# Attention: reciprocals of the softmax denominators taken once per value, in a 128x16 tile filled and spread by DMAs

## The chip, the core and the metric

The kernel runs on one NeuronCore of a Trainium2 chip. Its time is the device time of one execution in microseconds; three executions of the kernel before gave a median of 2079.34 us (2077.96 to 2079.47). A profile is of one execution, recorded by the hardware profiler. Engines: PE (TensorE: matmuls), DVE (VectorE), ACT (ScalarE), POOL (GpSimd), SP (SyncE, which here only issues DMAs).

## The reference

Two layers over x of shape (4, 1024, 512). The first is an adaptive-layernorm block with two MLPs. The second, cut to what matters here:

```python
h = _sln(hidden, w, ...)                                  # layernorm, scaled by the condition
q, k, v = ...                                             # 16 heads of 32, from h @ Wqkv.T + bqkv
energy = jnp.einsum('bhqd,bhkd->bhqk', q, k)              # 1024 x 1024 for each head and batch
att = jax.nn.softmax(energy, axis=-1) / D ** 0.5
out = jnp.einsum('bhqk,bhkd->bhqd', att, v)
out = out @ Wp.T + bp ; h1 = out + hidden ; return _sln(h1, ...) + h1
```

The softmax denominator of a query is one number for each head; the output of that query and head has 32 values, and all are divided by that one number.

## The kernel before

Five stages follow each other: setup, the first layer, the q/k/v projections, attention, and the output projection. Attention takes the stretch from about 950 to 1917 us. It works through 16 groups (4 batches x 4 groups of HG = 4 heads; 4 heads x 32 dimensions fill the 128 partitions). A group has STEPS = 16 steps: 2 halves of 512 queries, and in each half 8 blocks of 128 keys. Groups 1 to 12 run in a loop of 4 turns of 3 groups; the others are written out.

In a step PE makes four energy tiles (keys x queries, line 1149) in two PSUM banks, ACT takes their exponential (line 1278), and PE multiplies the one-step-older exponentials with v (line 1161, `av`). POOL adds the exponentials of two steps (line 1389, `pair`), and PE sums them over the keys with a stationary block of ones, 32 columns wide (line 1176, `den`): so each denominator stands 32 times, once for each of the 32 partitions of its head.

Beside it runs the search for the row maxima of queries that come later: 32 units to a group, two in each step. For a unit PE makes energies with queries on the partitions (line 1133, two matmuls of 512 keys) into one of two PSUM buffers `e_ps`, and DVE reduces them to a maximum (line 1305, `take_max`). Before the first matmul of unit n, PE waits until DVE has done unit n-2 (`pe.wait_ge(max_done, n - 1)`, line 1132). I call the two units of step i "ia" and "ib". The order is written out by hand: in an odd step PE also runs the first matmul of the next step's first unit (lines 1194 and 1195), behind the step's last energy tile. The units of steps 0 to 2 finish the group's own second half, those from step SWITCH = 3 belong to the next group. After them the maxima are negated, turned by PE and ACT, and put by two small DMAs as two more rows of the q stack (`place_neg`, line 1082).

At the end of a half ACT copies the sum of av to SBUF (`take_av`, line 1256), and later the denominators (`take_den`, line 1263: step 2 of the next group for half 1, step 10 for half 0). DVE inverts them in eight pieces of 128x64, one a step (`invert`, line 1324), between the step's two maxima. POOL multiplies (`finish`, line 1376), before pairs 1 and 5 of the next group, and SP stores the result to DRAM (`store`, line 1086).

All these DMAs go out on SP's one queue. In a group g, SP waits for the last av of group g-1 (in step 0), then issues ten loads for group g+2 (`load_group`: `load_stack` lines 90 and 94, nine DMAs, and v, line 1075; 3.5 MB; groups 1 to 13 only), then place_neg for half 1, store of half 0, place_neg for the next group's half 0, store of half 1. Group 15 loads the output projection's first inputs instead.

Of the kernel before, what the change touches and what calls it, by code (L numbers as in the profile page):

```python
# [6 lines left out]
P = 128  # L7
# [3 lines left out]
H, HD = 16, 32  # L11
KT = D // P
FT = FF // P
CH = 512
NCH = T // CH
TT = CH // P
G = B * KT
# [955 lines left out]
def attention_stage(nc, sh, wp_t):  # L973
# [11 lines left out]
    with ExitStack() as ctx:  # L985
        def sb(name, shape, dt=F32):
            return ctx.enter_context(nc.sbuf_tensor(name, shape, dt))

        def sem(name):
            return ctx.enter_context(nc.semaphore(name))  # L990
# [4 lines left out]
        LEAD = 13  # L995
        SWITCH = STEPS - LEAD
        TURN = (SWITCH + KC, SWITCH)
        PIECES = KC
        PC = CH // PIECES

        sh.projection_tiles = [t for t in early(nc, *PROJECTION_TILES) if "gap" not in t.name]
        sb("at_stacks_place", [P, 2 * RING * HG * N])
# [5 lines left out]
        av_sb = sb("at_av_sb", [P, QH, CH])  # L1008
        den_sb = sb("at_den_sb", [P, QH, CH])
        rden = sb("at_rden", [P, QH, CH])  # L1010
        out = sb("at_out", [P, QH, CH])
        mrow = sb("at_mrow", [P, QH, UNITS])
        neg = sb("at_neg", [P, 2, UNITS])
# [11 lines left out]
        av_done, av_taken = sem("at_av_done"), sem("at_av_taken")  # L1025
        pair_ready = sem("at_pair_ready")
        den_done, den_taken = sem("at_den_done"), sem("at_den_taken")
        rden_ready = sem("at_rden_ready")
        out_ready = sem("at_out_ready")
        wp_loaded, wp_split = sem("at_wp_loaded"), sem("at_wp_split")  # L1030

# [8 lines left out]
        def halves(g, h):  # L1040

            return QH * g + h + 1
# [25 lines left out]
        @block.sync  # L1068
        def _(sp):
            def load_group(g, slot):  # L1070
                load_stack(sp, sh, qs, ks, g, slot)
                load_v(g, slot)

            def load_v(g, slot):
                sp.dma_start(v[:, slot], sh.v_d[g]).then_inc(stack_loaded[slot], 16)

            def place_neg(g, slot, half):

                sp.wait_ge(negt_taken, halves(g, half))
                for part in range(2):  # L1080
                    dst = qs[96 + part:97 + part, slot, half].bitcast(F32).rearrange("o j (c q) -> o (j c) q", q=P)
                    sp.dma_start(dst, neg_t[part * UNITS:(part + 1) * UNITS, :]).then_inc(negm_loaded, 16)

            def store(g, half):
                sp.wait_ge(out_ready, halves(g, half))
                sp.dma_start(sh.at_d[g, :, half * CH:(half + 1) * CH], out[:, half]).then_inc(out_free[half], 16)

            def group(g, slot, nth=None, first=False, load=True, with_next=True):
                if not with_next:

                    sp.wait_ge(av_done, STEPS * g)
                    for half in range(QH):

                        sp.wait_ge(out_free[half], 16 * (KT + 1))
                    x, st = sh.projection_tiles[1], sh.projection_tiles[3]
                    for half in range(QH):
                        load_projection_input(sp, sh, a_f, x, st, 0, half)
                if not first and load:

                    sp.wait_ge(av_done, STEPS * g)  # L1100
                    load_group(g + 2, (slot + 2) % RING)
                place_neg(g, slot, 1)
                if not first:
                    store(g - 1, 0)
                if with_next:
                    place_neg(g + 1, (slot + 1) % RING, 0)
                if not first:
                    store(g - 1, 1)


            load_v(0, RING - 1)
            load_group(1, 0)
            place_neg(0, RING - 1, 0)
            load_group(2, 1)
            groups(sp, group)
            for half in range(QH):
                store(G - 1, half)

            for half in range(QH):
                sp.wait_ge(sh.a_loaded[half], 16 * KT)  # L1120
                sp.wait_ge(sh.x_loaded[half], 16)
                sp.wait_ge(sh.st_loaded[half], 32)
# [119 lines left out]
        def _(act):  # L1242
# [15 lines left out]
            def take_den(g, half):  # L1258
                act.wait_ge(den_done, KC // 2 * halves(g, half))
                if not (isinstance(g, int) and g == 0):  # L1260

                    act.wait_ge(rden_ready, PIECES * (halves(g, half) - 2))
                nc.scalar.copy(den_sb[:, half], den_ps[:]).then_inc(den_taken, 1)  # L1263

            def group(g, slot, nth=None, first=False, load=True, with_next=True):
# [36 lines left out]
        def _(dve):  # L1302
# [10 lines left out]
                dve.wait_ge(neg_ready, 2 * halves(g, half) - 1)  # L1313
                nc.vector.scalar_tensor_tensor(neg[:, LO, :], mrow[:, half], -1.0, neg[:, HI, :], ALU.mult, ALU.subtract).then_inc(neg_ready, 1)

            def invert(g, half, piece):

                if piece == 0:
                    dve.wait_ge(den_taken, halves(g, half))
                    if not (isinstance(g, int) and g == 0):  # L1320

                        dve.wait_ge(out_ready, halves(g, half) - 2)
                cols = slice(piece * PC, (piece + 1) * PC)
                nc.vector.reciprocal(rden[:, half, cols], den_sb[:, half, cols]).then_inc(rden_ready, 1)  # L1324

            def group(g, slot, nth=None, first=False, load=True, with_next=True):
                for i in range(STEPS):
                    units = units_of_step(g, slot, i, with_next)
                    for unit in units[0:1]:
                        take_max(*unit)  # L1330

                    if i >= 12:
                        for piece in ([i - 12] if with_next else [2 * (i - 12), 2 * (i - 12) + 1]):
                            invert(g, 0, piece)
                    elif not first:
                        invert(g - 1, *((1, i - 4) if i >= 4 else (0, i + 4)))
                    for unit in units[1:2]:
                        take_max(*unit)
                    if not with_next and KC // 2 <= i < KC // 2 + 2 * KT:

                        half, k = divmod(i - KC // 2, KT)
                        dve.wait_ge(sh.a_hi, KT * half + k + 1)
                        nc.vector.tensor_tensor(a_s[:, half, LO, k], a_f[:, half, k], a_s[:, half, HI, k].bitcast(F32),
                                                ALU.subtract).then_inc(sh.a_lo_last if k == KT - 1 else sh.a_lo, 1)
                    if i == TURN[1] - 1:
                        negate_max(g, 1)
                    if with_next and i == TURN[0] - 1:
                        negate_max(g + 1, 0)
# [8 lines left out]
                if n == UNITS - 1:  # L1357
                    negate_max(0, 0)
            groups(dve, group)
            for piece in range(PIECES):  # L1360
                invert(G - 1, 1, piece)

            dve.wait_ge(rden_ready, PIECES * halves(G - 1, 1))
            dve.wait_ge(av_taken, halves(G - 1, 1))
            dve.wait_ge(out_free[1], 16 * G)
            dve.wait_ge(out_ready, halves(G - 1, 0))
# [2 lines left out]
        @block.gpsimd  # L1369
        def _(pool):  # L1370
            def finish(g, half):
                pool.wait_ge(av_taken, halves(g, half))
                pool.wait_ge(rden_ready, PIECES * halves(g, half))

                pool.wait_ge(out_free[half], 16 * (g + 1))
                nc.gpsimd.tensor_tensor(out[:, half], av_sb[:, half], rden[:, half], ALU.mult).then_inc(out_ready, 1)

            def group(g, slot, nth=None, first=False, load=True, with_next=True):

                for pair in range(PAIRS if with_next else PAIRS - 1):  # L1380
                    if pair in (1, 5) and not first:
                        finish(g - 1, pair // 4)

                    pool.wait_ge(exp_done, HG * (STEPS * g + 2 * pair + 2))
                    if not (first and pair < 2):

                        pool.wait_ge(den_done, PAIRS * g + pair - 1)
                    a = 2 * pair % 4
                    nc.gpsimd.tensor_tensor(psum2[:, pair % 2], probs[:, a], probs[:, a + 1], ALU.add).then_inc(pair_ready, 1)  # L1389


            nc.gpsimd.memset(ks[96:98, 0:RING - 1].bitcast(F32), 1.0).then_inc(ones_ready, 1)
            pool.wait_ge(ones_ready, 1)
            pool.wait_ge(wp_split, 1)
            nc.gpsimd.tensor_tensor(sh.wp[:, LO], wp_raw[:], sh.wp[:, HI].bitcast(F32), ALU.subtract)
            groups(pool, group)
            finish(G - 1, 0)
# [234 lines left out]
def build(nc, x, cond_t, ada_w, wg_t, wb_t, row_bias, lngb, colpack, biasrows, neg_mask, ident, w1, w2, fw1, fw2, wqkv, wp_t, y,  # L1632
          stages=5):

    with ExitStack() as ctx:
# [11 lines left out]
        sh.bias_rows = sb("bias_rows", [2, D], F32R)  # L1647
        sh.minus_half = sb("minus_half", [P, TT])
        sh.eps = sb("eps", [P, 2, TT])
        sh.act_passed, sh.dve_passed, sh.pe_passed = (ctx.enter_context(nc.semaphore(f"{e}_passed")) for e in ("act", "dve", "pe"))  # L1650
        sh.biasrows_in = biasrows
        sh.rows_d = nc.dram_tensor("rows_scratch", [len(SPREAD), B, D], F32, kind="Internal").ap()
        sh.x2_d = nc.dram_tensor("x2_scratch", [T, D], F32, kind="Internal").ap()

        sh.qk_d = nc.dram_tensor("qk_scratch", [2, 2, G, P, N], F32, kind="Internal").ap()
        sh.v_d = nc.dram_tensor("v_scratch", [G, P, KC, P], F32, kind="Internal").ap()
        sh.at_d = nc.dram_tensor("attn_scratch", [G, P, N], F32, kind="Internal").ap()

        weights = [w1.rearrange("(k p) n -> p k n", p=P), w2.rearrange("(k p) n -> p k n", p=P)]
# [78 lines left out]
```

## Time and profile before

| | us |
|---|---|
| median of 3 runs | 2079.34 (2077.96 to 2079.47) |
| span of the profiled execution, first to last instruction | 2077.5 |
| PE busy / DVE busy / POOL busy / ACT busy | 1964.5 / 1383.0 / 1105.7 / 855.7 |
| the reciprocals, line 1324 | 136.8 |

The profiled execution has no time of its own beside its span; the span lies 1.8 us under the median. "Busy" is the time in which an engine worked on an instruction. Matmuls overlap each other, so their start times say more than their durations.

### The profile page before, as it was taken

What the parts mean: (1) busy time and instruction counts of PE and PEld (TensorE: products, weight loads), DVE (VectorE), ACT (ScalarE), POOL (GpSimd) and SP (SyncE); (2) the same over time, 40 slices, a digit from 0 to 9 for tenths busy, and PEclk for the clock granted to TensorE, in tenths of its full rate; (3) what the DMA queues carried; (4) which work ended last, traced back from release to release, by engine and by line L of the source; (5) the groups of instructions that cost most, each with busy time, mean ns of one, the idle gap of its engine ahead of it and who ended that gap; (6) DMA issues with size and microseconds to landing.
All of it is one profiled execution on the core that took longest, in us unless ns stands there. A gap on an engine that the chain in (4) does not pass through costs nothing. (4 is left out here: it accounts for less than half of the span.)

```text
span 2077.5 us, 29213 instructions
## 1 busy us (share of the span) xinstructions
PE 1964.5 (95%) x9504; PEld 1203.7 (58%) x9504; DVE 1383.0 (67%) x1754; ACT 855.7 (41%) x1469; POOL 1105.7 (53%) x553
## 2 busy tenths in 40 slices
PE   6599999999998999989999999999999999998974
PEld 1488888888887888864444444444444444442652
DVE  3555665566455544447788778778777878876678
ACT  1323112311222222214666566656656666665212
POOL 0675556555652121223666666666665666665655
PEclk9799999999999999987999999999999999999987
DMA  7300101110125554664332133333213333021454
GB/s 238 111 31 22 51 30 40 30 50 20 31 102 183 177 187 177 207 186 93 77 82 49 41 83 77 82 83 74 51 47 83 77 83 83 11 83 59 139 166 147
DMA packets 104341, 189.24 MB, mean 91 GB/s; under 512 B 8186, under 2 KB 25722, under 8 KB 104220
## 3 DMA queue, kind: packets, MB, share of 16 engines
q1 hardware_dynamic: 85472, 176.71, 29.6%
q10 hardware_dynamic: 18560, 10.94, 1.8%
q8 instruction: 71, 1.16, 0.2%
q14 instruction: 46, 0.38, 0.1%
q0 software_dynamic: 192, 0.05, 0.0%
HBM read 119.99 MB, written 67.16 MB: 90 GB/s over the span
## 5 line engine op out<-in xcount | busy, mean ns | idle before, releaser
L1305 DVE TENSOR_REDUCE at_mrow<-banks 128x1 f32<-128x1024 f32 x512 | 614.7, 1222 | 198.1 <-PE banks L1133 198.1
L1389 POOL TENSOR_TENSOR at_pair<-at_probs 128x2048 f32<-128x2048 f32 x127 | 581.3, 4577 | 294.6 <-ACT at_probs L1278 294.6
L1278 ACT ACTIVATE at_probs<-banks 128x512 f32<-128x512 f32 x1024 | 556.9, 595 | 329.2 <-PE banks L1149 321.6
L1149 PE MATMUL banks<-early_qs,early_ks 98*128 98x512 f32 x1024 | 454.5, 447 | 11.3 <-issue 8.7
L1149 PEld LDWEIGHTS banks<-early_qs,early_ks 98*128 98x128 f32 x1024 | 193.0, 190 | 397.9 <-ACT at_probs L1278 350.5
L1133 PE MATMUL banks<-early_ks,early_qs 96*128 96x512 f32 x1024 | 399.0, 415 | 6.3 <-PEq L726 3.5
L1161 PE MATMUL banks<-at_probs,at_v 128*32 128x512 f32 x2048 | 276.2, 612 | 0.9 <-ACT at_probs L1278 0.9
L1133 PEld LDWEIGHTS banks<-early_ks,early_qs 96*128 96x128 f32 x1024 | 199.0, 197 | 46.4 <-DVE at_mrow L1305 19.5
L66 PE MATMUL banks<-l_ht,l_weights 128*128 128x512 f32 x768 | 178.8, 392 | 5.6 <-ACT l_gt L546 5.6
L66 PE MATMUL banks<-qk_nt,l_weights 128*128 128x512 f32 x768 | 177.1, 392 | 3.0 <-ACT qk_gt L861 3.0
L546 ACT ACTIVATE l_gt<-banks,mod 128x512 f32<-128x512 f32 x64 | 48.1, 777 | 313.9 <-PE banks L440 278.1
L66 PE MATMUL banks<-l_weights,l_hf 128*128 128x512 f32 x768 | 177.2, 390 | 0.0
L66 PEld LDWEIGHTS banks<-l_ht,l_weights 128*128 128x128 f32 x768 | 144.5, 189 | 35.8 <-issue 6.0
L66 PEld LDWEIGHTS banks<-qk_nt,l_weights 128*128 128x128 f32 x768 | 145.2, 189 | 33.5 <-ACT qk_gt L861 3.2
L66 PEld LDWEIGHTS banks<-l_weights,l_hf 128*128 128x128 f32 x768 | 143.7, 188 | 29.5
L1324 DVE RECIPROCAL at_rden<-at_den_sb 128x64 f32<-128x64 f32 x256 | 136.8, 539 | 14.2 <-ACT at_den_sb L1263 14.2
L1176 PE MATMUL banks<-at_pair,at_ones_col 128*32 128x512 f32 x1016 | 135.7, 606 | 0.0
L960 POOL TENSOR_TENSOR qk_nt<-qk_gt,qk_nt 128x512 fp32r<-128x512 f32 x32 | 43.0, 1362 | 156.3 <-DVE qk_nt L912 156.3
L870 ACT ACTIVATE qk_out<-banks,cols 128x512 fp32r<-128x512 f32 x64 | 44.1, 690 | 192.5 <-PE banks L66 186.4
L672 POOL TENSOR_TENSOR l_ht<-l_gt,l_ht 128x512 fp32r<-128x512 f32 x64 | 84.1, 1314 | 63.1 <-DVE l_ht L588 63.1
L588 DVE CAST l_ht<-l_gt 128x512 fp32r<-128x512 f32 x64 | 52.0, 812 | 90.3 <-ACT l_gt L555 49.0
L555 ACT ACTIVATE l_gt<-banks,cols 128x512 f32<-128x512 f32 x96 | 64.6, 688 | 105.0 <-POOL l_hf L672 51.0
(124 smaller groups left out, 2069.4 us busy)
## 6 DMA issues: line engine op xcount, KB each, us to landing
qk_scratch<-qk_out SPq DMA_DIRECT2D x64, 512.0 KB, 2.9
early_ks<-qk_scratch SPq DMA_DIRECT2D x48, 512.0 KB, 6.7
early_qs<-qk_scratch SPq DMA_DIRECT2D x96, 256.0 KB, 11.3
v_scratch<-qk_v ACTq DMA_DIRECT2D x32, 256.0 KB, 2.4
at_v<-v_scratch SPq DMA_DIRECT2D x16, 512.0 KB, 14.9
attn_scratch<-at_out SPq DMA_DIRECT2D x32, 256.0 KB, 2.3
o_a<-attn_scratch SPq DMA_DIRECT2D x32, 256.0 KB, 6.4
o_x<-x_scratch SPq DMA_DIRECT2D x8, 1024.0 KB, 7.4
```

The source lines that it names most:

```text
L66: last = pe.matmul(out, stationary(a), moving(b), start=start and n == 0, stop=stop and n == len(TERMS) - 1)
L555: nc.scalar.activation(gt[:, n % 2, :], halves[n][:], func, bias=sh.cols[:, col + m:col + m + 1]).then_inc(gt_full, 1)
L588: nc.vector.tensor_copy(dst[:, HI, i, :], gt[:, i % 2, :]).then_inc(gt_hi, 1)
L672: nc.gpsimd.tensor_tensor(dst[:, LO, i, :], gt[:, i % 2, :], dst[:, HI, i, :].bitcast(F32), ALU.subtract).then_inc(gt_lo, 1)
L1133: pe.matmul(e_ps[u % 2][:, keys, :], qs[0:96, slot, half, j, c * P:(c + 1) * P], ks[0:96, slot, j, keys * CH:(keys + 1) * CH], start=True, ...
L1149: pe.matmul(et[j % 2][:], ks[0:98, slot, j, (i % KC) * P:(i % KC + 1) * P], qs[0:98, slot, i // KC, j, :], start=True, stop=True).then_inc ...
L1161: last = pe.matmul(av_ps[rows, :], v[:, slot, kc, rows], probs[:, kc % 4, j, :], start=kc == 0, stop=kc == KC - 1)
L1176: last = pe.matmul(den_ps[rows, :], ones_col[:], psum2[:, pair % 2, j, :], start=n == 0, stop=n == KC // 2 - 1)
L1278: nc.scalar.activation(probs[:, i % 4, j, :], et[j % 2][:], ACT.Exp).then_inc(exp_done, 1)
L1305: nc.vector.tensor_reduce(mrow[:, half, u:u + 1], e_ps[u % 2], AX.XY, ALU.max).then_inc(max_done, 1)
L1324: nc.vector.reciprocal(rden[:, half, cols], den_sb[:, half, cols]).then_inc(rden_ready, 1)
L1389: nc.gpsimd.tensor_tensor(psum2[:, pair % 2], probs[:, a], probs[:, a + 1], ALU.add).then_inc(pair_ready, 1)
```

## The change

The denominators no longer are inverted in all their 32 copies. From `den_sb` a DMA takes one row of each head (4 rows of 512 values) and lays them out as 128 partitions x 16 values (`den_c`). DVE inverts this tile with one instruction. SP stores it to DRAM, waits until it has landed there, and loads it back with four DMAs, each of which writes a head's 512 values to 32 partitions of `rden`. The order on SP, DVE and POOL changes with it. The last half of the last group is inverted whole, without DMAs.

```diff
+        DEN_STEP = 2
+        ROWS = P // HG
+        DW = CH // ROWS
...
+            def spread_den(g, half):
+                sp.wait_ge(den_taken, halves(g, half))
+                if not (isinstance(g, int) and g == 0):
+                    sp.sem_inc(sh.sp_passed, 1)
+                    sp.wait_ge(rden_ready, halves(g, half) - 2)
+                sp.sem_inc(sh.sp_passed, 1)
+                sp.dma_start(den_c[:, half],
+                             den_sb[0:P:HD, half].rearrange("j (r c) -> j r c", c=DW)).then_inc(den_spread[half], 16)
+
+            def widen_rden(g, half):
+                first = isinstance(g, int) and g == 0
+                sp.wait_ge(rden_ready, halves(g, half))
...
+                sp.dma_start(sh.rden_d[half].rearrange("j (r c) -> (j r) c", c=DW), rden_c[:, half]).then_inc(rden_stored[half], 16)
+                sp.wait_ge(rden_stored[half], 16 * (g + 1))
...
+                    sp.wait_ge(out_ready, halves(g, half) - 2)
...
+                for j in range(HG):
+                    sp.dma_start(rden[HD * j:HD * (j + 1), half],
+                                 sh.rden_d[half, j].partition_broadcast(HD)).then_inc(rden_loaded[half], 16)
...
                     sp.wait_ge(av_done, STEPS * g)
                     load_group(g + 2, (slot + 2) % RING)
+                if not first:
+                    store(g - 1, 0)
+                    spread_den(g - 1, 1)
                 place_neg(g, slot, 1)
                 if not first:
-                    store(g - 1, 0)
+                    widen_rden(g - 1, 1)
+                    store(g - 1, 1)
+                spread_den(g, 0)
                 if with_next:
                     place_neg(g + 1, (slot + 1) % RING, 0)
-                if not first:
-                    store(g - 1, 1)
-
+                widen_rden(g, 0)
...
 # ACT, take_den
-                    act.wait_ge(rden_ready, PIECES * (halves(g, half) - 2))
+                    act.wait_ge(den_spread[half], 16 * g)
...
 # DVE
-            def invert(g, half, piece):
...
-                nc.vector.reciprocal(rden[:, half, cols], den_sb[:, half, cols]).then_inc(rden_ready, 1)
+            def invert(g, half):
+                dve.wait_ge(den_spread[half], 16 * (g + 1))
+                if not (isinstance(g, int) and g == 0):
+                    dve.wait_ge(rden_stored[half], 16 * g)
+                nc.vector.reciprocal(rden_c[:, half], den_c[:, half]).then_inc(rden_ready, 1)
 
                 for i in range(STEPS):
-                    units = units_of_step(g, slot, i, with_next)
-                    for unit in units[0:1]:
+                    for unit in units_of_step(g, slot, i, with_next):
                         take_max(*unit)
-
-                    if i >= 12:
-                        for piece in ([i - 12] if with_next else [2 * (i - 12), 2 * (i - 12) + 1]):
-                            invert(g, 0, piece)
-                    elif not first:
-                        invert(g - 1, *((1, i - 4) if i >= 4 else (0, i + 4)))
-                    for unit in units[1:2]:
-                        take_max(*unit)
+                    if i == DEN_STEP + 2 and not first:
+                        invert(g - 1, 1)
+                    if i == KC + DEN_STEP + 2:
+                        invert(g, 0)
...
-            for piece in range(PIECES):
-                invert(G - 1, 1, piece)
+            nc.vector.reciprocal(rden[:, 1], den_sb[:, 1]).then_inc(rden_ready, 1)
...
 # POOL, finish and group
-                pool.wait_ge(rden_ready, PIECES * halves(g, half))
+                pool.wait_ge(rden_loaded[half], 16 * HG * (g + 1))
...
-                    if pair in (1, 5) and not first:
-                        finish(g - 1, pair // 4)
+                    if pair == 3 and not first:
+                        finish(g - 1, 1)
+                    if pair == PAIRS - 1:
+                        finish(g, 0)
```

## Rows read from the trace of the kernel before

**Rows 1.** The page, busy time of each engine: us (share of the span) xinstructions.
```profile
PE 1964.5 (95%) x9504; PEld 1203.7 (58%) x9504; DVE 1383.0 (67%) x1754; ACT 855.7 (41%) x1469; POOL 1105.7 (53%) x553
```
**Rows 2.** Busy times by stretch; a plain group, then one with the loop's turn.
```profile
1253.00:1312.00 59.00, 59.00 (x326) 25.53 (x322) 47.48 (x53) 37.00 (x71) 39.03 (x11) 1.00 0.32 73
1371.00:1435.00 64.00, 61.88 (x322) 26.57 (x322) 46.90 (x52) 36.93 (x70) 38.88 (x10) 0.95 0.29 68
```
**Rows 3.** Waits, PE's and DVE's, 1000 to 1910 us: total, times, longest.
```profile
PE banks L1149 <- issue: 8.7, 3, 3.1
PE banks L1149 <- ACT at_probs L1278: 2.5, 6, 0.5
DVE at_mrow L1305 <- PE banks L1133: 180.5, 321, 3.0
```
**Rows 4.** The page's groups of instructions: busy, mean ns | idle before, releaser.
```profile
L1305 DVE TENSOR_REDUCE at_mrow<-banks 128x1 f32<-128x1024 f32 x512 | 614.7, 1222 | 198.1 <-PE banks L1133 198.1
L1324 DVE RECIPROCAL at_rden<-at_den_sb 128x64 f32<-128x64 f32 x256 | 136.8, 539 | 14.2 <-ACT at_den_sb L1263 14.2
```
**Rows 5.** Timeline, loads of group 5, then group 6: start, duration, engine, line.
```profile
1254.15 1.36 SPq L90 DMA_DIRECT2D early_ks<-qk_scratch  x3
...
1313.26 1.37 SPq L90 DMA_DIRECT2D early_ks<-qk_scratch  x3
1317.78 0.38 SPq L1075 DMA_DIRECT2D at_v<-v_scratch  x1
1322.69 0.58 ACT L1263 COPY at_den_sb<-banks 128x512 f32<-128x512 f32 x1 [0.73 <-PE banks L1176]
1329.05 1.22 DVE L1305 TENSOR_REDUCE at_mrow<-banks 128x1 f32<-128x1024 f32 x1 [0.38 <-PE banks L1133]
1331.19 1.23 DVE L1305 TENSOR_REDUCE at_mrow<-banks 128x1 f32<-128x1024 f32 x1 [0.92 <-PE banks L1133]
1332.89 0.64 PE L1133 MATMUL banks<-early_ks,early_qs 96*128 96x512 f32 x2
1333.86 4.58 POOL L1389 TENSOR_TENSOR at_pair<-at_probs 128x2048 f32<-128x2048 f32 x1 [2.47 <-ACT at_probs L1278]
```
**Rows 6.** DMA issues of group 6 by line, and their landing times from issue.
```profile
L1075 SPq DMA_DIRECT2D at_v<-v_scratch x1: 381/381/381, 1317.8 to 1317.8; - x1
DMA to landing us min/median/max: 13.5/13.5/13.5
L1082 SPq DMA_DIRECT2D early_qs<-at_neg_t x2: 508/545/582, 1326.6 to 1327.1; - x2
DMA to landing us min/median/max: 4.9/5.4/5.9
L1086 SPq DMA_DIRECT2D attn_scratch<-at_out x1: 430/430/430, 1327.9 to 1327.9; - x1
DMA to landing us min/median/max: 5.4/5.4/5.4
```
**Rows 7.** The same small DMAs and store in group 14, which loads nothing.
```profile
L1082 SPq DMA_DIRECT2D early_qs<-at_neg_t x2: 502/546/590, 1810.3 to 1810.8; - x2
DMA to landing us min/median/max: 1.8/1.8/1.8
L1086 SPq DMA_DIRECT2D attn_scratch<-at_out x1: 578/578/578, 1811.5 to 1811.5; - x1
DMA to landing us min/median/max: 2.2/2.2/2.2
```
**Rows 8.** Timeline at a turn of the loop, in the attention.
```profile
1373.12 0.79 PE L1149 MATMUL banks<-early_qs,early_ks 98*128 98x512 f32 x1 [2.64 <-issue]
1374.70 1.94 PE L1161 MATMUL banks<-at_probs,at_v 128*32 128x512 f32 x8
1376.99 1.38 SPq L90 DMA_DIRECT2D early_ks<-qk_scratch  x3
```
**Rows 9.** Timeline at the end of attention, DVE.
```profile
1911.85 3.43 DVE L1324 RECIPROCAL at_rden<-at_den_sb 128x64 f32<-128x64 f32 x8 [14.22 <-ACT at_den_sb L1263]
```

More of the change, by code:

```diff
@@ L997, in attention_stage @@
         TURN = (SWITCH + KC, SWITCH)
-        PIECES = KC
-        PC = CH // PIECES
+        DEN_STEP = 2
+        ROWS = P // HG
+        DW = CH // ROWS
         sh.projection_tiles = [t for t in early(nc, *PROJECTION_TILES) if "gap" not in t.name]
@@ L1010, in attention_stage @@
         rden = sb("at_rden", [P, QH, CH])
+        den_c = sb("at_den_c", [P, QH, DW])
+        rden_c = sb("at_rden_c", [P, QH, DW])
         out = sb("at_out", [P, QH, CH])
@@ L1027, in attention_stage @@
         den_done, den_taken = sem("at_den_done"), sem("at_den_taken")
+        den_spread = [sem(f"at_den_spread{i}") for i in range(QH)]
         rden_ready = sem("at_rden_ready")
+        rden_stored = [sem(f"at_rden_stored{i}") for i in range(QH)]
+        rden_loaded = [sem(f"at_rden_loaded{i}") for i in range(QH)]
         out_ready = sem("at_out_ready")
@@ L1082, in place_neg @@
                     sp.dma_start(dst, neg_t[part * UNITS:(part + 1) * UNITS, :]).then_inc(negm_loaded, 16)
+            def spread_den(g, half):
[10 more added lines that the diff above has]
+                if not first:
+                    sp.sem_inc(sh.sp_passed, 1)
+                    sp.wait_ge(rden_loaded[half], 16 * HG * g)
+                sp.sem_inc(sh.sp_passed, 1)
+                sp.dma_start(sh.rden_d[half].rearrange("j (r c) -> (j r) c", c=DW), rden_c[:, half]).then_inc(rden_stored[half], 16)
+                sp.wait_ge(rden_stored[half], 16 * (g + 1))
+                if not first:
+                    sp.sem_inc(sh.sp_passed, 1)
+                    sp.wait_ge(out_ready, halves(g, half) - 2)
+                sp.sem_inc(sh.sp_passed, 1)
+                for j in range(HG):
+                    sp.dma_start(rden[HD * j:HD * (j + 1), half],
+                                 sh.rden_d[half, j].partition_broadcast(HD)).then_inc(rden_loaded[half], 16)
             def store(g, half):
@@ L1101, in group @@
                     load_group(g + 2, (slot + 2) % RING)
+                if not first:
+                    store(g - 1, 0)
+                    spread_den(g - 1, 1)
                 place_neg(g, slot, 1)
                 if not first:
-                    store(g - 1, 0)
+                    widen_rden(g - 1, 1)
+                    store(g - 1, 1)
+                spread_den(g, 0)
                 if with_next:
                     place_neg(g + 1, (slot + 1) % RING, 0)
-                if not first:
-                    store(g - 1, 1)
+                widen_rden(g, 0)
             load_v(0, RING - 1)
@@ L1314, in negate_max @@
                 nc.vector.scalar_tensor_tensor(neg[:, LO, :], mrow[:, half], -1.0, neg[:, HI, :], ALU.mult, ALU.subtract).then_inc(neg_ready, 1)
-            def invert(g, half, piece):
[L1318 to L1323, printed above, removed]
-                nc.vector.reciprocal(rden[:, half, cols], den_sb[:, half, cols]).then_inc(rden_ready, 1)
+            def invert(g, half):
[3 more added lines that the diff above has]
+                nc.vector.reciprocal(rden_c[:, half], den_c[:, half]).then_inc(rden_ready, 1)
             def group(g, slot, nth=None, first=False, load=True, with_next=True):
                 for i in range(STEPS):
-                    units = units_of_step(g, slot, i, with_next)
-                    for unit in units[0:1]:
+                    for unit in units_of_step(g, slot, i, with_next):
                         take_max(*unit)
-                    if i >= 12:
-                        for piece in ([i - 12] if with_next else [2 * (i - 12), 2 * (i - 12) + 1]):
-                            invert(g, 0, piece)
-                    elif not first:
-                        invert(g - 1, *((1, i - 4) if i >= 4 else (0, i + 4)))
-                    for unit in units[1:2]:
-                        take_max(*unit)
+                    if i == DEN_STEP + 2 and not first:
+                        invert(g - 1, 1)
+                    if i == KC + DEN_STEP + 2:
+                        invert(g, 0)
                     if not with_next and KC // 2 <= i < KC // 2 + 2 * KT:
@@ L1359, in _ @@
             groups(dve, group)
-            for piece in range(PIECES):
-                invert(G - 1, 1, piece)
-            dve.wait_ge(rden_ready, PIECES * halves(G - 1, 1))
+            dve.wait_ge(den_taken, halves(G - 1, 1))
+            dve.wait_ge(out_ready, halves(G - 1, 1) - 2)
+            nc.vector.reciprocal(rden[:, 1], den_sb[:, 1]).then_inc(rden_ready, 1)
+            dve.wait_ge(rden_ready, halves(G - 1, 1))
             dve.wait_ge(av_taken, halves(G - 1, 1))
@@ L1649, in build @@
         sh.eps = sb("eps", [P, 2, TT])
-        sh.act_passed, sh.dve_passed, sh.pe_passed = (ctx.enter_context(nc.semaphore(f"{e}_passed")) for e in ("act", "dve", "pe"))
+        sh.act_passed, sh.dve_passed, sh.pe_passed, sh.sp_passed = (ctx.enter_context(nc.semaphore(f"{e}_passed")) for e in ("act", "dve", "pe", "sp"))
         sh.biasrows_in = biasrows
@@ L1656, in build @@
         sh.v_d = nc.dram_tensor("v_scratch", [G, P, KC, P], F32, kind="Internal").ap()
+        sh.rden_d = nc.dram_tensor("rden_scratch", [QH, HG, CH], F32, kind="Internal").ap()
         sh.at_d = nc.dram_tensor("attn_scratch", [G, P, N], F32, kind="Internal").ap()
```

## The prediction, made before the changed kernel was run

> **What bounds the kernel now.** I read the page's busy times first: PE works 95% of the span, DVE 67% [rows 1]. A busy share is an average, so I looked at attention alone. In a plain group PE is busy all of its 59 us at full clock, DVE 47 of them [rows 2]. The waits say it more sharply: from 1000 to 1910 us PE waits 8.7 us in three pieces for "issue", at the loop's three turns back, and 2.5 us for ACT; no wait for DVE is among them, while DVE waits 180 us for PE [rows 3]. So PE sets the pace, and DVE has time to spare: on average, not at any moment. The units of maxima hang together in both directions, through two PSUM buffers. What matters is how late DVE may be in one place before PE stops. A stop of PE isn't made good, as it has no idle time in which to catch up.
>
> **The work removed.** The 256 pieces are 136.8 us of DVE, with 0.43 us from start to start where they follow each other (8 in 3.43 us) [rows 4, 9]. Thirty-one of the 32 halves are now inverted by one 128x16 instruction. Per column a piece costs 0.43/64 = 0.007 us; 48 columns fewer than its 0.54 us give 0.54 - 0.32 = 0.22 us [rows 4, 9]; I take that. DVE is relieved of about 125 us. All of it lies beside PE's work, so it's worth nothing until PE waits for DVE. The cover is safe: PE has no wait that this DVE work ended. At attention's very end the 8 pieces are on the path; one 128x512 instruction at the same rate per column is the same 3.4 us, at most 0.3 less. I count 0.
>
> **The wait added, where it costs.** DVE now waits at step 4 of group g for the DMA that lays out the denominators of (g-1, half 1). Queued behind the waiting instruction on DVE are the maxima from 5a on; PE waits for those. Times of group 6 [rows 5, 6]:
> - The ten loads start at 1313.26, the last (v) is issued at 1317.78 and lands 13.5 us later, at 1331.3. The queue is full until then.
> - ACT has the denominators in SBUF at 1322.69 + 0.58 = 1323.3, so SP issues the layout there. Ahead of it in the same queue are the loads and, new, the store of half 0 (256 KB), which used to come after place_neg.
> - What does a small DMA do behind that queue? The two of place_neg, 8 KB each, were issued at 1326.6 and 1327.1 and landed 4.9 to 5.9 us later, both near 1332.0 to 1332.5; with nothing ahead they land in 1.8 us [rows 7]. So they did wait for the loads. The store behind them landed at 1327.9 + 5.4 = 1333.3.
> - The layout now stands behind loads and store. Lower bound: both store and layout move in no time, 1332.5. Upper bound: the store's 1333.3 and 0.9 us more for 128 pieces of 64 bytes, 1334.2. No row shows such small pieces; I take 1333.2, next to the store's landing, because the place in the queue is that of the store, and both small DMAs that stood before it are gone.
> - DVE is there at 1329.05 + 1.22 = 1330.3. It inverts at 1333.2 and is free at 1333.4, where 5a started at 1331.19: 2.2 us late. 5a then ends at 1334.65.
> - PE needs 5a for the first matmul of 6a, the second of the two from 1332.89 on, which started at about 1333.13. It now starts at 1334.65: a stop of 1.5 us. Bounds: 0.8 us by 1332.5, 2.5 us by 1334.2.
>
> The Trainium skill ("DMA: Bandwidth & Descriptors", section "Why a DMA increments its semaphore by 16 and not by 1") says that a DMA runs on as many of the 16 engines as divide the outermost dimensions of both sides. By it the layout (4 rows to 128 partitions) has 4 engines, each with 32 pieces, and is slower in itself than a transfer on all 16; the sum would lean to its upper end. No row here shows a DMA on four engines.
>
> **How often.** Groups 1 to 13 load. Place_neg's landing, counted from its issue, hardly differs in eleven of them (5.8 to 6.3 us against 5.9 here); in groups 7 and 13 it was about 1 us earlier. So 13 x 1.5 = 19.5, less about 1.5: 18 us. Group 14 has an empty queue: store 2.2 us, small DMA 1.8 us [rows 7], landed before DVE comes, 7 us after the denominators (1330.3 against 1323.3 [rows 5]). In group 15 no maxima are left to take after step 2; DVE's wait there holds only the splitting of the projection's input. I count 0 for both, with 1 us of doubt.
>
> **What else moves, at nothing.** Half 0: its layout is issued at step 10 into a queue that has long been empty, and lands 1.8 to 2.5 us later, while DVE comes two steps (7.4 us) after. Place_neg is now behind up to one store and one layout, some 1 to 2 us later, and is needed only at step 8, over 10 us after group 6's 1332.5. The widening for half 1: inverse at 1333.4, store to DRAM 0.4 + 2.2, four issues of 0.45 and a landing of 2.3, ready near 1340.3. POOL's pair 2 runs to 1333.86 + 4.58 = 1338.4 [rows 5], and pair 3 can't start before step 7's exponentials near 1341 (or 1342.5 with PE's stop): `finish`, 1.3 us, fits to within 1 us. ACT needs pair 3 only at step 10. SP's longer list delays nobody: its next urgent work is the loads at the next group's step 0, and widening half 0 is over some 5 us before. If that cover were gone, the price is the overrun itself, once a group.
>
> **The sum.** 2077.5 + 18 = 2095.5 for the profiled execution; the median lies 1.8 above the span, giving 2097.5, say 2098 us.
>
> **The rivals.**
> 1. *PE's clock falls with the stops* (chance 0.17). At the loop's turn PE stopped for 2.64 us and then ran its av of 8 matmuls in 1.94 us instead of 1.06; the stretch's granted clock is 0.95 [rows 2, 8]. From group 5's loads to group 6's it is 59.1 us, from group 6's (1313.26) to the turn's (1376.99) 63.7 [rows 5, 8]: 4.6 more, of which 2.6 are the stop, so the low clock (1.2 instead of 2.4 GHz) cost 2.0. If each stop brings this, 13 x (1.5 + 2.0) less 2 gives 43 us: 2122. Against it: my stop is half as long, and the only ones followed by a low clock in attention are the turns. It decides where stops come to 2.5 us. The Trainium skill ("TensorE: Matmul & The Clock Gate", "What's actually happening") has the low clock as PE's default, which activity lifts: by that rule a PE busy before and behind a stop of 1.5 us can keep its clock, and the sum stays at 2098.
> 2. *Not slower: the layout lands in time* (0.14: 0.10 for no difference, 0.04 for faster). If small DMAs pass the bulk of the queue, or the loads end a microsecond earlier, the layout lands by 1331.65: then DVE ends 5a by 1333.1 and PE doesn't notice. Time 2079, at best 2078 if the lighter DVE removes a few of the short waits. It decides at 1331.65, 0.85 us under my lower bound. For it speaks only that 4 of 16 queues may be drained earlier than the last one, which the landings show; against it, place_neg in thirteen groups.
> 3. *Widening is late as well* (0.04). If store and reload take 5 us more than counted, POOL's pair 3 slips and ACT and PE with it, about 2 us in 15 groups: 2128.
>
> **How the numbers follow.** My forecast, 0.65, has its own range from 13 x 0.6 to 13 x 2.5: 2087 to 2112. Rival 1 reaches above, rival 2 below. From 2083 to 2125 about 0.8 is held: rival 2 and the tail of rivals 1 and 3 stay out. A difference under 0.2% (4 us) can't be told from none here: faster 0.04, same 0.10, slower 0.86.
>
> **What would show it.** In the changed trace: DVE's line 1305 or the reciprocal with 13 waits for a DMA into `at_den_c` of 2 to 3 us; the first layout DMA landing about 10 us after its issue in loading groups and about 2 us in group 14 and for half 0; PE's line 1133 waiting for DVE `at_mrow`, 13 times 1.5 us; the granted clock still 1.00 between the turns. I'm wrong if the layout lands within 8.3 us of its issue, if PE's wait for DVE stays under 5 us in all, or if the clock rows show falls beside the turns.

## The result and the profile after

The changed kernel took 2089.07 us (median of 20 runs) against 2078.84 us: ratio 1.0049, 95% interval 1.0039 to 1.0058. It is slower by 10 us, where 18 us was forecast. The profiled execution has a span of 2086.1 us, 8.6 more than before.

The page's busy times, which answer to [rows 1]:

```profile
PE 1965.9 (94%) x9504; PEld 1204.3 (58%) x9504; DVE 1270.6 (61%) x1530; ACT 855.6 (41%) x1469; POOL 1105.5 (53%) x553
```

DVE is relieved of 112 us, and the kernel is slower all the same. The waits of 1000 to 1910 us, answering to [rows 3] (engine, its line <- what it waited for: total, times, longest; PEld is PE's weight load, which waits with its matmul):

```profile
PE banks L1186 <- issue: 8.7, 3, 3.2
PE banks L1170 <- DVE at_mrow L1342: 6.6, 11, 1.2
PE banks L1186 <- ACT at_probs L1315: 2.4, 6, 0.5
PEld banks L1170 <- DVE at_mrow L1342: 12.0, 12, 1.6
DVE at_rden_c L1358 <- DMA at_den_c<-at_den_sb: 34.9, 14, 7.6
```

Line 1170 is the maxima's matmul (1133 before), line 1342 the maximum, line 1358 the inversion. The second and the last row are new. Of the 34.9 us the longest piece, 7.6, is in group 15, where no maxima are left; without it 13 waits of 2.1 us remain, one for each loading group. The timeline of group 6 shows how such a wait becomes a stop (answers to [rows 5]):

```profile
1328.34 0.62 SPq L1097 DMA_DIRECT2D at_den_c<-at_den_sb  x1
1333.99 1.23 DVE L1342 TENSOR_REDUCE at_mrow<-banks 128x1 f32<-128x1024 f32 x1 [0.83 <-PE banks L1170]
1337.12 0.25 DVE L1358 RECIPROCAL at_rden_c<-at_den_c 128x16 f32<-128x16 f32 x1 [1.90 <-DMA at_den_c<-at_den_sb]
1337.29 3.45 DVE L1342 TENSOR_REDUCE at_mrow<-banks 128x1 f32<-128x1024 f32 x3
1337.82 0.40 PE L1170 MATMUL banks<-early_ks,early_qs 96*128 96x512 f32 x1
1338.50 0.50 PE L1170 MATMUL banks<-early_ks,early_qs 96*128 96x512 f32 x1 [0.28 <-DVE at_mrow L1342]
```

The denominators were in SBUF at 1328.17. DVE ends 4b at 1335.22 and stands for 1.90 us, until the layout DMA, issued 8.8 us before, has landed. Then it takes three maxima without a pause. The first of them, 5a, holds back the last row, 6a's first matmul: PE begins it 0.68 us after the matmul before, where back-to-back ones are 0.24 us apart.

The trace gives this for each of the 13 loading groups. From the end of ACT's copy (line 1300) to 6a's first matmul it was 9.78 to 9.86 us in all of them before. Now it is 10.76, 10.18, 11.22, 11.02, 10.72, 10.33, 9.89, 10.40, 10.29, 10.96, 10.56, 10.28 and 10.49: against 9.85, stops of 0.70 us on average, 9.1 us together. In group 14, which loads nothing, it is 9.86. So the stops make up the whole 8.6 us of the span. The inversion began 8.2 to 9.8 us after the denominators, 9.14 on average.

The busy times of a plain group and one with the loop's turn, answering to [rows 2]; the third column from the end is the granted clock:

```profile
1259.00:1318.00 59.00, 58.33 (x321) 25.02 (x319) 40.04 (x38) 36.30 (x69) 38.19 (x11) 1.00 0.36 82
1318.00:1382.00 64.00, 60.54 (x326) 25.99 (x322) 41.03 (x39) 37.21 (x70) 42.22 (x11) 0.97 0.32 76
```

PE's clock is full between the turns, as before. At the end of attention, answering to [rows 9]:

```profile
1920.39 3.35 DVE L1391 RECIPROCAL at_rden<-at_den_sb 128x512 f32<-128x512 f32 x1 [17.60 <-ACT at_den_sb L1300]
```

It is 3.35 us for the one instruction, against 3.43 for the eight pieces: 0.08 us saved.

### The profile page after: what moved, and what is told of

It is laid out like the page before. It is cut to its first block and busy times, and to the rows that moved or that the text cites. A ratio compares the mean times of both kernels' runs of the same rounds, so it can differ in the third digit from the quotient of the medians.

```text
span 2086.1 us, 29394 instructions
## 1 busy us (share of the span) xinstructions
PE 1965.9 (94%) x9504; PEld 1204.3 (58%) x9504; DVE 1270.6 (61%) x1530; ACT 855.6 (41%) x1469; POOL 1105.5 (53%) x553
## 5 line engine op out<-in xcount | busy, mean ns | idle before, releaser
L66 PE MATMUL banks<-wp,o_as 128*128 128x512 f32 x384 | 105.5, 428 | 0.0
## 6 DMA issues: line engine op xcount, KB each, us to landing
at_v<-v_scratch SPq DMA_DIRECT2D x16, 512.0 KB, 14.3
```

What stands on the lines that cost most here:

```text
L66: last = pe.matmul(out, stationary(a), moving(b), start=start and n == 0, stop=stop and n == len(TERMS) - 1)
```

## The experiments

All ratios are to the kernel before, run on the same chip. Each edit is made to the changed kernel, unless the text says otherwise. "Stops" are counted as above: how much later than 9.85 us after the denominators 6a's first matmul begins, summed over the 13 loading groups.

**Invert later.** Two edits of the changed kernel:

```diff
-                    if i == DEN_STEP + 2 and not first:
+                    if i == DEN_STEP + 4 and not first:
                         invert(g - 1, 1)
...
-                    if pair == 3 and not first:
+                    if pair == 4 and not first:
                         finish(g - 1, 1)
```

> As the changed kernel, but DVE inverts half 1 of the previous group at step 6 instead of step 4, and POOL's finish of it comes before pair 4 instead of pair 3. Theory A (the loss is DVE standing before the layout DMA at step 4, so that PE's first matmul of unit 6a waits, 13 groups of about 0.7 us): at step 6, some 14 us after the denominators, the layout has long landed (about 9 us after them); no wait of DVE for at_den_c but in group 15, PE's waits for DVE at_mrow fall by about 7 us, ratio to before 1.000 (2077 to 2081 us). Theory B (the loss comes from elsewhere: the additional DMAs, POOL's new place for finish, SP's order): the ratio stays near 1.005.

Ratio 0.9998 (0.9989 to 1.0007). Its waits, same stretch and columns:

```profile
PE banks L1186 <- issue: 9.1, 3, 3.1
PE banks L1186 <- ACT at_probs L1315: 2.5, 6, 0.5
DVE at_rden_c L1358 <- DMA at_den_c<-at_den_sb: 0.3, 1, 0.3
```

PE no longer waits for DVE. Every added DMA is still there, and so is POOL's late finish. The stops are gone too (6a's matmul at 9.86 to 9.89). Theory A holds: the place of one wait is the whole loss. Theory B falls.

**Invert one step later only.**

```diff
-                    if i == DEN_STEP + 2 and not first:
+                    if i == DEN_STEP + 3 and not first:
```

> As the changed kernel, but half 1 is inverted after the maxima of step 5 instead of 4; POOL's finish stays before pair 3. DVE reaches it 10.7 us or more after the denominators, where the layout has landed by 9.8 in all groups: no stops of PE, ratio 1.000 to 1.0005. Against it: the widened reciprocals come about 1.5 us later than in the changed kernel, and POOL's finish before pair 3 may then hold pair 3 by up to 1 us; if ACT and PE feel that, the ratio stays at 1.002 or more.

Ratio 1.0001 (0.9992 to 1.001); PE's waits for DVE are gone, DVE's for the layout are 2.0 us in one piece. One step is enough. POOL now stands before the widened reciprocals for 18.4 us in 12 pieces, 1.7 at most, and ACT and PE don't feel it.

**The store behind place_neg.**

```diff
                 if not first:
-                    store(g - 1, 0)
                     spread_den(g - 1, 1)
                 place_neg(g, slot, 1)
                 if not first:
+                    store(g - 1, 0)
                     widen_rden(g - 1, 1)
```

> As the changed kernel, but the store of half 0 is issued after place_neg, so that it doesn't stand before the layout in the queue. Theory A with the store as part of the delay: the layout lands about 0.7 us sooner (8.5 instead of 9.2 us after the denominators), PE's stops fall from 0.7 to about 0.1 us, ratio 1.001. Rival (the place behind the ten loads alone, or the slowness of the layout itself, makes the delay): landing hardly moves, ratio stays 1.004 to 1.005.

Ratio 1.0018 (1.0009 to 1.0027), expected 1.001. Waits:

```profile
PE banks L1170 <- DVE at_mrow L1342: 2.0, 3, 1.1
PEld banks L1170 <- DVE at_mrow L1342: 5.6, 10, 1.5
DVE at_rden_c L1358 <- DMA at_den_c<-at_den_sb: 26.5, 14, 6.5
```

The inversion began 8.6 us after the denominators on average, 0.5 sooner. The stops fell from 9.1 to 3.4 us (6a's matmul at 11.14 in the worst group, at 9.90 or less in six). The store was over half of the loss.

**Store and v behind place_neg.** As before, and `load_v(g + 2, ...)` moved from `load_group` to the line ahead of the store.

> As the changed kernel, but both the load of v (512 KB) and the store of half 0 (256 KB) are issued after place_neg, so only the nine loads of q and k stand before the layout; DVE still inverts at step 4. Theory A (the place in the queue sets the loss): without store the layout landed about 8.6 us after the denominators, without v another 1.2 us sooner, 7.4 us; DVE comes at 7.05, PE needs it by 8.4: no stop, DVE's waits for at_den_c under 0.6 us a group, ratio 1.000 to 1.0005. Rival (what DVE waits for is mostly the layout's own length on its few engines): stops of at least 0.3 us stay, ratio 1.002 as with the store moved alone.

Ratio 1.0001 (0.9992 to 1.001). PE waits for DVE once, 0.3 us, with a weight load; DVE still waits for the layout, but is through in time:

```profile
DVE at_rden_c L1360 <- DMA at_den_c<-at_den_sb: 16.1, 12, 7.3
```

Without group 15's 7.3 us that is 0.8 us a time, a little more than the 0.6 expected, and free: the inversion began 7.7 us after the denominators on average, and PE needs 5a only later. The wait stands at step 4 and costs nothing if the queue is shorter. The queue is not all of the landing time, though. The trace has the time of each increment of a DMA's semaphore, which I call a count: in group 6 of this kernel the layout's last piece had ended at 6.3 us after the denominators and its last count came at 7.8, 1.5 us later, where it was 0.45 us in the changed kernel. What holds the count back here stays open.

**The queue made longer.** After the store and ahead of the layout (and once before the first group, so that the counts fit):

```diff
                     store(g - 1, 0)
+                    sp.wait_ge(extra, 16 * g)
+                    sp.dma_start(extra_d, wp_raw[:, 0]).then_inc(extra, 16)
                     spread_den(g - 1, 1)
```

> As the changed kernel, with one more DMA of 256 KB to a scratch area in DRAM ahead of the layout in groups 1 to 15 (one more before the first group). Theory A: the layout lands about 0.7 us later, each of the 13 stops grows by as much, about 9 us more: ratio to before 1.009 (2097 to 2100 us). Theory B: the ratio stays near 1.005. If the longer stops bring PE's low clock, the ratio is 1.012 or more.

Ratio 1.0092 (1.0076 to 1.0107), as theory A had it. PE's waits for DVE:

```profile
PE banks L1177 <- DVE at_mrow L1349: 11.7, 13, 1.6
PEld banks L1177 <- DVE at_mrow L1349: 17.4, 13, 2.0
```

The ratio is the one expected, partly by luck, for the stops are smaller: the inversion began 9.6 us after the denominators on average, 0.4 us later than in the changed kernel and not 0.7. The stops are 14.3 us in the profile, 1.1 us each instead of 1.4, and there is one fall of PE's clock for 3.4 us after the longest of them (1.8 us), 1.7 us more (half of 3.4). That leaves about 1 us of the span's 16.9 open, and some 2 us more of the ratio's 19 us.

**The longer queue, inverted at step 6.** Both edits together.

> The kernel with the additional 256 KB ahead of the layout, and with half 1 inverted at step 6 and finished before pair 4. Theory A: the longer queue costs only through DVE's wait at step 4; with the wait moved it costs nothing, ratio 1.000. Rival (the additional DMA traffic itself costs part of the 19 us): 1.002 or more.

Ratio 0.9999 (0.999 to 1.0008). The same traffic is worth 19 us with the wait at step 4 and nothing with it at step 6. So the additional traffic by itself costs nothing that can be told (the rival's 1.002 lies outside the interval).

**DVE's relief alone.** In the kernel before (the edit also sets all of `rden` to 1 once, ahead of the attention):

```diff
+                cols = slice(piece * PC, piece * PC + 16)
                 nc.vector.reciprocal(rden[:, half, cols], den_sb[:, half, cols]).then_inc(rden_ready, 1)
```

> The kernel before, with its eight pieces kept, but each piece inverts only 16 of its 64 columns; the others keep the value 1, so most of the output isn't divided by its denominator. It shows what DVE's relief alone (some 80 us less) is worth. Theory A: nothing, PE never waited for DVE: ratio 1.000 (2079 to 2081 us). Rival (the lighter DVE gives back a few us, and the wait costs more than the 9 us seen): 0.998 or less.

Ratio 0.9993 (0.9984 to 1.0002): no difference that can be told; if there is a gain, it's at most about 3 us. DVE's busy time fell by 75 us (to 1307.6), two thirds of the changed kernel's 112.

**The layout on all engines.** (DVE and ACT then wait for four DMAs' counts instead of one's; those two lines are left out.)

```diff
-                sp.dma_start(den_c[:, half],
-                             den_sb[0:P:HD, half].rearrange("j (r c) -> j r c", c=DW)).then_inc(den_spread[half], 16)
+                for j in range(HG):
+                    sp.dma_start(den_c[HD * j:HD * (j + 1), half],
+                                 den_sb[HD * j:HD * j + 1, half].rearrange("j (r c) -> j r c", c=DW)).then_inc(den_spread[half], 16)
```

> As the changed kernel, but the layout is four DMAs, one for each head (1 row to 32 partitions), instead of one with 4 rows to 128 partitions. If the forecast was too long because the layout runs on few engines and so need not wait for the one engine of 16 that an instruction fetch holds up, then the four DMAs on all engines land later, about 9.9 us after the denominators as the store did in the kernel before; stops of 1.4 us, ratio 1.009. Rival (the layout's own 32 pieces on an engine are what takes time, and spreading them helps): landing about 8.8, stops of 0.3 us, ratio 1.002.

Ratio 1.0214 (1.02 to 1.0228): later, as the first theory has it, but by far more than it said. Group 6, and busy times of the stretch from group 5's denominators to group 6's:

```profile
1357.34 0.25 DVE L1359 RECIPROCAL at_rden_c<-at_den_c 128x16 f32<-128x16 f32 x1 [4.05 <-DMA at_den_c<-at_den_sb]
1358.73 0.50 PE L1171 MATMUL banks<-early_ks,early_qs 96*128 96x512 f32 x1 [2.42 <-DVE at_mrow L1343]
```

```profile
1283.00:1346.00 63.00, 60.62 (x323) 25.92 (x322) 40.39 (x39) 37.04 (x71) 38.91 (x11) 0.97 0.34 76
```

The denominators were there at 1346.26, so the inversion began 11.1 us after them (expected 9.9). The times of the DMA packets in the trace, all counted from the denominators here, say why it is late at all: of the 128 pieces of 64 bytes 120 had begun by 8.7 us, the last eight only at 9.9 to 10.0. An instruction fetch of 16 KB had run from 7.8 to 8.9, and the last rows of the store ended at 9.9. I read this as one engine held up by the fetch, with the store's rows and its share of the layout queued behind. In the changed kernel the same fetch ran in group 6 (7.6 to 8.6), but all pieces of the layout had begun by 8.5.

That the layout there did not run on the late engine is shown by the semaphores. The store of half 0, ahead of the layout in the same queue, landed behind it:

```profile
L1120 SPq DMA_DIRECT2D attn_scratch<-at_out x1: 383/383/383, 1323.4 to 1323.4; - x1
DMA to landing us min/median/max: 14.8/14.8/14.8
```

That is 1338.2, and DVE was inverting from 1337.12 on. Count by count: 15 of the store's 16 counts had come by 8.8 us after the denominators and the last at 10.05, while the layout's came at 8.62, 8.84, 8.88 and 8.92 (one more at 1.2 us, before any piece had moved). In 12 of the 13 loading groups the layout's last count came before the store's. The 13th is a control for the fetch: there the fetch began only at 8.3 us, when the store's rows were nearly through, and the store's last count came with the others, at 8.94.

The counts also say why the inversion began 1.1 us after the last piece here, against 0.5 us in the changed kernel. The four DMAs give 64 counts; 60 had come by 9.87 us, the last four at 10.59, 10.75, 10.91 and 11.06. The eight late pieces are two of each DMA, so I take these for the late engine's counts, one for each DMA, 0.16 us apart.

The rest of the excess is PE's clock. The span grew by 49.3 us over the kernel before; the stops add up to 29.0. Apart from the turns the granted clock fell to 1.2 GHz eight times, each time between 0.4 us before and 1.3 us after the end of a stop, for 3.4 or 6.8 us and 37.4 in all: half of that, 18.7 us, is lost. At the turns it was low for 17.1 us in all against 13.7 before, 1.7 us lost. The three make 49.4. In the stretch shown, 63.2 us passed from denominators to denominators against 59.1 before: 2.6 of stop and 1.5 of a clock that was low for 3.4 us. Of the nine stops of 2.36 to 2.79 us eight had a fall at their end (group 6's, of 2.62, is the one without), of the four from 1.2 to 2.2 us none.

## Why the prediction was right, and where its size was off

- *PE sets the pace, the relief is worth nothing*: right. The relief alone gives 0.9993 (0.9984 to 1.0002), the end of attention 0.08 us. The relief itself was taken too large, 125 us against 112 in the page's busy time: the 136.8 us are a sum of durations that overlap (eight of 0.54 us took 3.43).
- *The wait at step 4, in the queue behind loads and store, 13 groups*: right, in place and number. Moved by a step it costs nothing; with the queue made longer it costs 19 us instead of 10 by the ratios (14.3 us of stops instead of 9.1).
- *"I take 1333.2, next to the store's landing"*: this term was mis-sized. It put the landing 9.9 us after the denominators; DVE began to invert 8.95 us after them in group 6 and 9.14 on average. Even the lower bound of 1332.5, 9.2 us, was not one: in 8 of 13 groups DVE began sooner. It came from a reading that pairs rows crosswise: place_neg's two DMAs, issued at 1326.6 and 1327.1, landed 4.9 and 5.9 us later, at 1331.5 and 1333.0, and not "both near 1332.0 to 1332.5". In the trace before 30 of their 32 counts had come by 8.5 us after the denominators (1331.8), the last two at 9.5 and 9.7; of the store's 16, 15 by 8.7 and the last at 10.1. So both landings that the forecast leaned on are those of one late count in 16, in group 6 by the reading above that of the engine with the instruction fetch (7.3 to 8.5 us in that kernel), on which the layout had no piece. For the sum the forecast used the Trainium skill's rule on the number of engines ("DMA: Bandwidth & Descriptors", "Why a DMA increments its semaphore by 16 and not by 1") only for 32 pieces on each, so slower. The trace agrees with the four engines (four late counts), but the 128 pieces took 0.5 us, and what the small number does here is the opposite. The forecast had this in view, as what speaks for rival 2 (four of 16 may be drained earlier), and gave it no part in the sum. The experiment with four DMAs on more engines agrees in sign.
- *A stop of 1.5 us*: 0.70. Nearly all of the difference is the landing, 0.8 us sooner on average. From the inversion's start to 6a's matmul it was 1.41 us on average, against the 1.45 taken.
- *13 x 1.5 less 1.5 = 18 us*: 9.1 us of stops in the profile, 8.6 in the span, 10 in the medians. That the time still lies in the range is in part luck: the range starts at 13 x 0.6, though the stop's own lower bound was 0.8, above the 0.70 measured, and the prediction gives no reason for the 0.6. (The sum of 2095.5 and 1.8 is 2097.3, not 2097.5; nothing hangs on it.)
- *Groups 14 and 15, half 0, place_neg, the widening and POOL at nothing*: right. DVE's wait of 7.6 us in group 15 is there and costs nothing. POOL waits once, 2.9 us, for the widened tile, also in the kernel with the store moved; the kernel that inverts at step 5 keeps finish before pair 3 and loses nothing. So rival 3 did not come about either.
- *Rival 1, the clock*: not in this kernel, whose stops are 1.4 us at most. But it's real, about where it was put (stops of 2.5 us): eight of nine stops of 2.36 us and more had it in the kernel with four layout DMAs, and one of 1.8 us in the kernel with the longer queue. *Rival 2, in time*: its condition (landing by 1331.65, 8.4 us) held in one group only, group 7, at 8.2; the stop there is 0.04 us.

## What to carry to other kernels

An engine with a third of its time idle can still stop the one that bounds, if it waits in the wrong place: ask when each operand of an in-order engine lands, not how busy the engine is. A small DMA on which an engine waits lands when what stands ahead of it, on the DMA engines that it uses, is through. Here it was enough to issue 768 KB of the bulk behind it, or to put the wait one step later: the price was zero. When you take a landing time from another DMA's row, ask whether both run on the same engines: the landing of a DMA on all 16 is that of the last one.

## What the runs showed that was not expected

A 16 KB instruction fetch ran for 1.1 us on the DMA engines in group 6 of all three kernels looked at above, and the DMAs on 16 engines ended about that much later on one of them, while the one layout DMA was not touched. Four DMAs in place of one, for the same 8 KB, made the inversion begin 1.6 us later on average (10.7 against 9.1) and the kernel about 34 us slower than the changed one by the ratios. In the profiled executions it is 41 us: 20 by longer stops and 20 by PE's clock, so that a stop of 2.4 to 2.8 us with a fall of the clock at its end cost 4.8 us on average, twice its length.
